# First attention of a fused graph kernel: layer-norm statistics of batches 2 to 7 made early, GpSimd's normalisations cut into pieces of three tiles

## What is computed

```python
x = x + _L0_gnn_ref(_layernorm(x, axis=-1), adj, L0_gnn_W, L0_gnn_a)      # the first attention
x = x + _L0_ffn_ref(_layernorm(x, axis=-1), ...)                          # 2 of 8 experts for each row
x = x + _L1_gnn_ref(_layernorm(x, axis=-1), adj, a0, a1, a2, a3)
x = x + _L1_ffn_ref(_layernorm(x, axis=-1), ...)

def _L0_gnn_ref(input, adj, W, a):
    h = jnp.matmul(input, W)
    f1, f2 = h @ a[:128, 0], h @ a[128:, 0]
    e = leaky_relu(f1[:, :, None] + f2[:, None, :], 0.2)
    attention = softmax(jnp.where(adj > 0, e, -9e15), axis=1)
    return elu(matmul(attention, h))
```

## Time and profile before

| | us |
|---|---|
| median of 3 runs | 1229.13 |
| lowest and highest run | 1223.91, 1231.8 |
| the profiled execution | 1227.33 |
| its span | 1225.6 |
| of it the loop of the first attention, from the first `shift` to the last | 34.3 to 315.0 |

### The profile page before, as it was taken

How to read it: one execution, slowest core, us unless ns; L and a number is a source line. 1 busy time by engine, 2 the same in 40 slices (tenths; PEclk the granted TensorE clock), 3 DMA queues, 4 the chain that set the end, 5 groups by cost and what they waited for, 6 DMA issues and landing times. The chain is left out here.

```text
span 1225.6 us, 17486 instructions
## 1 busy us (share of the span) xinstructions
PE 1119.4 (91%) x5314; PEld 672.3 (55%) x5346; DVE 671.1 (55%) x2158; ACT 743.4 (61%) x1063; POOL 414.1 (34%) x483
## 2 busy tenths in 40 slices
PE   2998898999619999969999999999799999999998
PEld 2554454444317777747777777777444444444443
DVE  4788987886634435436666667653253333333325
ACT  3887787786205554536666666666466666566661
POOL 6237777766755040434454555211000000000000
PEclk9898998998759999989999999999899999999999
DMA  8886765762134466422222222210000000000001
GB/s 260 319 322 217 276 215 211 254 233 108 39 126 130 140 191 190 141 78 78 80 79 79 78 79 81 66 52 11 1 0 9 9 17 9 18 9 9 18 9 35
DMA packets 69134, 130.98 MB, mean 107 GB/s; under 512 B 9918, under 2 KB 30764, under 8 KB 68012
## 3 DMA queue, kind: packets, MB, share of 16 engines
q1 hardware_dynamic: 60268, 111.96, 27.7%
q0 software_dynamic: 8192, 16.79, 4.6%
q10 hardware_dynamic: 576, 1.05, 0.2%
HBM read 77.60 MB, written 52.17 MB: 106 GB/s over the span
## 5 line engine op out<-in xcount | busy, mean ns | idle before, releaser
L1907 DVE CUSTOM_DVE_ANT_0 f_Y<-f_T,f_R 128x1024 f32<-128x1024 f32 x64 | 78.3, 1223 | 121.6 <-ACT f_R L1864 121.6
L2087 PE MATMUL eU<-XTN,V 128*128 128x512 f32 x256 | 133.5, 604 | 6.2 <-PEq L2021 6.2
L553 PE MATMUL O<-Y,HS 128*128 128x512 f32 x256 | 137.9, 660 | 0.0
L2095 PE MATMUL eU<-H,V 128*128 128x512 f32 x256 | 131.6, 596 | 0.0
L2103 PE MATMUL eY<-dGW,Vo 128*128 128x512 f32 x256 | 130.3, 596 | 1.3 <-DVE dGW L2294 1.2
L1746 POOL DMA_INDIRECT W<-sorted_y,ROW_I x96 | 91.5, 953 | 114.7 <-PE f_T L1807 96.6
L411 POOL DMA_INDIRECT sorted_x<-V,AT_I x112 | 110.6, 988 | 45.8 <-issue 29.7
L2194 ACT ACTIVATE H<-eU,bn 128x512 f32<-128x512 f32 x128 | 99.7, 779 | 39.5 <-PE eU L2087 32.5
L1827 PEld LDWEIGHTS f_O<-f_XN,f_PT 128*128 128x128 f32 x896 | 108.2, 192 | 17.8 <-issue 16.4
L1801 PE MATMUL f_T<-f_XT,f_XTA 128*128 128x512 f32 x224 | 114.6, 593 | 2.3 <-DVE f_XTA L1976 0.8
L1878 ACT COPY f_PT<-f_TP 128x512 f32<-128x512 f32 x128 | 68.8, 589 | 74.7 <-PE f_TP L1817 74.7
(11 more groups left out here) (281 smaller groups left out, 2011.8 us busy)
## 6 DMA issues: line engine op xcount, KB each, us to landing
ADJ<-in_adj SPq DMA_DIRECT2D x64, 512.0 KB, 5.1
masks<-NM SPq DMA_DIRECT2D x8, 2048.0 KB
f_MK<-masks SPq DMA_DIRECT2D x60, 256.0 KB, 2.7
sorted_y<-zero SPq DMA_DIRECT2D x39, 256.0 KB, 10.6
XB<-sorted_x SPq DMA_DIRECT2D x39, 256.0 KB, 2.7
sorted_y<-YB SPq DMA_DIRECT2D x39, 256.0 KB, 2.2
X<-in_x SPq DMA_DIRECT2D x8, 512.0 KB, 7.9
out_x<-X SPq DMA_DIRECT2D x16, 256.0 KB, 2.3
```

The source lines that it names most:

```text
L553: pe.matmul(O[:, h * HALF:(h + 1) * HALF], HS[:, g % 3, :], Y[:, g % 4, h * HALF:(h + 1) * HALF], start=False, stop=(c == NT - 1)).then_in ...
L1907: v.tensor_tensor_reduce(Y[:, g % 3, :], T[g % 2][:, :], R4[:, g % 2, :], -SLOPE, 3.0e38, ALU.add, ALU.min, LOW[:, g % RING:g % RING + 1]) ...
L2087: pe.matmul(U1[j % 2][:, :], V1[:, e * P:(e + 1) * P], XTN[:, b * N + q * HALF:b * N + (q + 1) * HALF], start=True, stop=True).then_inc(u1 ...
L2095: pe.matmul(U2[j % 2][:, :], V2[:, e * P:(e + 1) * P], H1[:, j % 2, :], start=True, stop=True).then_inc(u2_ready, 1)
```

## The change

LESS, SPREAD and ROOT get eight buffers in place of two, one per batch. The six `stats(2)` to `stats(7)` move: they stood in slot 1 of batches 0 to 5 (g = 1, 9, 17, 25, 33, 41) and now stand at g = 1, 3, 5, 7, 8 and 9. The wait of `stats` for `xn_ready` goes with the buffers.

On POOL, `norm(b + 2)` is cut: ROOT stays in slot 1, the eight tiles of XN go as three, three and two into slots 2, 3 and 4, behind the pair of scatters of each slot. `norm_r(b - 1)` is cut as well: `root_r` stays in slot 5, tiles 0 to 2 go to slot 6, 3 to 5 to slot 7, 6 and 7 to slot 0 of the next batch. The last `norm_r(7)` stays whole. No computation is added or left out.

```diff
-            LESS, SPREAD, ROOT, LESS_R, SPREAD_R, ROOT_R = (tile(n, [P, 2, NT]) for n in (
-                "LESS", "SPREAD", "ROOT", "LESS_R", "SPREAD_R", "ROOT_R"))
+            LESS, SPREAD, ROOT = (tile(n, [P, B, NT]) for n in ("LESS", "SPREAD", "ROOT"))
+            LESS_R, SPREAD_R, ROOT_R = (tile(n, [P, 2, NT]) for n in ("LESS_R", "SPREAD_R", "ROOT_R"))
...
-                def norm(b):
+                def root(b):
                     pool.wait_ge(mv_ready, b + 1)
-                    g_.tensor_tensor(ROOT[:, b % 2, :], SPREAD[:, b % 2, :], half8, ALU.pow).then_inc(pstep, 1)
+                    g_.tensor_tensor(ROOT[:, b, :], SPREAD[:, b, :], half8, ALU.pow).then_inc(pstep, 1)
                     pool.wait_ge(pstep, steps.next())
-                    if b >= 1:
-                        pool.wait_ge(xnt_ps[1], b)
-                    for t in range(NT):
...
+                def norm(b, tiles):
+                    for t in tiles:
+                        if t == 0 and b >= 1:
+                            pool.wait_ge(xnt_ps[1], b)
...
-                def norm_r(b):
-                    pool.wait_ge(root_ready, b + 1)
-                    if b >= 2:
-                        pool.wait_ge(sent[b % 2], b // 2 * EACH)
-                    for t in range(NT):
+                def norm_r(b, tiles):
+                    for t in tiles:
+                        if t == 0:
+                            pool.wait_ge(root_ready, b + 1)
+                            if b >= 2:
+                                pool.wait_ge(sent[b % 2], b // 2 * EACH)
...
                         send(sending, (2 * k, 2 * k + 1))
+                    if c == 0 and b >= 2:
+                        norm_r(b - 2, (6, 7))
                     if c == 1 and b + 2 < B:
-                        norm(b + 2)
+                        root(b + 2)
+                    if c in (2, 3, 4) and b + 2 < B:
+                        norm(b + 2, ((0, 1, 2), (3, 4, 5), (6, 7))[c - 2])
                     if c == 5 and b >= 1:
                         root_r(b - 1)
-                        norm_r(b - 1)
+                    if c in (6, 7) and b >= 1:
+                        norm_r(b - 1, ((0, 1, 2), (3, 4, 5))[c - 6])
...
                 send(LAST - 2, (2 * NT - 2, 2 * NT - 1))
+                norm_r(LAST - 1, (6, 7))
...
                 def stats(b):
                     moments(b)
-                    if b >= 2:
-                        dve.wait_ge(xn_ready, b - 1)
...
-                    if c == 1 and b + 2 < B:
-                        if b == 0:
-                            dve.wait_ge(x_rest, 16 * (B - 2))
-                        stats(b + 2)
+                    if g == 1:
+                        dve.wait_ge(x_rest, 16 * (B - 2))
+                    if g in (1, 3, 5, 7, 8, 9):
+                        stats((1, 3, 5, 7, 8, 9).index(g) + 2)
```

## The result

Before, in this comparison: 1228.32 us median (1223.73 to 1235.8, 20 runs). After: 1233.22 us (1226.89 to 1243.55, 20 runs). The ratio is 1.0042, 95% interval 1.0022 to 1.0062: slower by some 5 us, inside the 1% that I called "same" and inside the range, but on the other side of zero from the forecast of -1.7. The profiled execution has a span of 1229.5 us against 1225.6.

The account below looks back on a forecast made before the run. TensorE, busy 91% of the span, was taken to bound the kernel, with VectorE nearly as full in the loop. The terms -5.76 + 0 + 3.79 + 0.3 = -1.67 us took the 1229.13 median to 1227.5, range 1220.5 to 1236.

Parts of the forecast that it names:

- the 1% that I called "same": Whole kernel: a change within about 1%, 12.3 us, can't be told from none; chance of "same" 0.92.
- Part 3: POOL's norms in pieces: 0 in the loop, covered by POOL's idle time; +0.3 us in the tail.
- the Trainium skill's rule on the port: VectorE and GpSimd lock a shared port pair; read as longer cut tiles on POOL, up to +1.4 us in the tail.
- Part 1: `stats` leaving slot 1 of batches 2 to 5: -5.76 us in batches 4 and 5, 1.20 pacing and 4.56 clock.
- "0" for batches 2 and 3: Removing `stats` there is worth 0: the `shift` behind waited anyway, and the clock falls begin in untouched waits.
- Part 2: Four more `stats` between slots 3 and 9: 10.04 us of VectorE work less 6.25 idle, +3.79 us.
- no `shift` from 5 to 9 waits: Sign of being right: no `shift` from 5 to 9 waits for R.
- a sign against itself: A low clock between 50 and 80 us would show the forecast wrong.
- The tail: POOL's work up to `root_r(7)`, with `norm_r(6)` cut in three: +0.3 us, bounds -0.5 and +1.4.
- the estimated 0.1 for each start: In the tail, three starts of `norm_r(6)` in place of one cost an estimated 0.1 us each.
- A: Clock falls in batches 0 and 1, or batches 4 and 5 keep theirs: slower, 1232.0 to 1235.0 us; chance 0.30.
- B with Part 2 fully hidden: All clock falls go, batches 2 and 3 included (1222.3 us, chance 0.20); with the added `stats` hidden too, -10.3.

Follow-up runs that it names:

- e13: The changed kernel measured once more on a chip at 1229: ratio 1.0044 to the kernel before; its loop took 291.8 us.
- e1: The changed kernel with POOL's two norms whole again, only the statistics early: 4.8 us faster than the kernel before, ratio 0.9961.
- e17: Early statistics with both norms whole, measured again on another chip, at 1229: 1.5 us faster than the kernel before, ratio 0.9988.
- e2: The changed kernel with `stats` put back to slot 1, only POOL's norms in pieces: 3.4 us slower than the kernel before.
- e4: The kernel before without statistics 4 to 7, norms using those of batches 2 and 3: 0.66% faster, 8.1 us.
- e14: The changed kernel with the second norm whole in slot 5, the first in pieces, on a chip at 1229: level with the kernel before.
- e16: The changed kernel with the scatters of slots 2 and 3 held back, six in a row in slot 4: ratio 1.0018 to the kernel before.
- e3: The kernel before with four more sets of statistics added into a spare tile, nothing taken away: 0.44% slower, 5.4 us.
- e8: Early statistics, norms whole, later batches' statistics in halves in slots 1 and 3: 26.30 us from shift 3 to 10; no gain in time, chip at 1254.
- e12: The changed kernel with the first norm whole, the second in pieces, on a chip where the kernel before took 1259; the text gives no time.

## Why the prediction was wrong, step by step

The loop by groups of batches, each trace against the trace of before, in us (batch 7 up to its last `shift`):

```
batches             0, 1    2, 3    4, 5     6       7     loop
forecast            +3.8     0      -5.8     0       0     -2.0
changed kernel      +4.9    -0.6    -3.3    +1.0    -0.5   +1.5
  again (e13)       +8.2    -0.7    -3.3    +5.7    +1.3  +11.1
early alone (e1)    +5.4    -3.2    -4.3    +0.2    -3.2   -5.1
  again (e17)       +4.1    -3.2    -4.3    +0.2    -3.2   -6.4
```

**Part 3, "In the loop I count 0": this step failed.** It asked only whether anybody waits for POOL's results, and nobody does. But the pieces put a tile right behind a scatter 27 times between the start of batch 2 and the last `shift`, where the kernel before and e1 never do, and small operations of VectorE beside such a scatter take 0.52 in place of 0.17 to 0.23. These are on the path: they make H's parts and CH. Read against e1, slot 4 costs 0.64 more in two batches, slot 7 0.36 to 0.57 in five. In batch 4, where no trace of either kernel has a low clock, that leaves 35.36 and 35.37 (after, e13) against 34.52 and 34.51 (e1, e17). TensorE waits 9.2 us for CH from batch 2 to the last `shift` in place of 6.5 in e1, and more low clock comes with it: 27.3 and 50.8 us of the loop in the two traces with pieces, 17.1 and 23.5 in e1 and e17. How much of the clock is due to the pieces is not shown. Behind early statistics the pieces cost 7 to 10 us on the chips at 1230 (1.0042 and 1.0044 against 0.9961 and 0.9988, intervals that touch at most), each ratio against before on its own chip; the two kernels never ran side by side on such a chip. Alone the pieces cost 3.4 (e2), not clear of zero.

The prediction had the Trainium skill's rule on the port that VectorE and GpSimd share ("SBUF — State Buffer", SBUF: two separate sides) in hand and turned it one way only, to longer tiles on POOL. The trace shows the other: the 32 XN tiles of batches 2 to 5 took 18.6 us together where they took 20.2 before, and VectorE's operations were held. That the shared port is the cause no run shows.

**Part 1, batches 4 and 5 (-5.76): right for batch 4, too large for batch 5.** The falls of the clock in slot 3 of both batches (187.6 and 225.1 us in the trace of before) are gone with the `stats` of slot 1, as forecast, and e4 shows the full amount. With early statistics, however, another fall comes in slot 0 of batch 5: 212.3 to 215.8 us in e1, 211.0 to 214.4 in e17, 215.4 to 218.8 in the changed kernel. Batch 5 then takes 36.36 in e1 and 36.31 in e17, not 34.70. So some 1.6 us of this term failed without the pieces, and 0.8 in batch 4 through them. Why that fall comes is open: e14 and e16, with early statistics too, do not have it.

**"0" for batches 2 and 3: a right number by luck.** 75.59 before, 74.96 after. e1 shows what is under it: the earlier statistics alone bring 3.2 us there, and the pieces take 2.5 of them back.

**Part 2, four more `stats` (+3.79): right.** From shift 3 to shift 10 it is 3.7 after, 3.5 in e1, 3.3 in e3, and no `shift` from 5 to 9 waits. Batches 0 and 1 together grew by more, 4.9, with the two falls of the clock (54.9 and 72.0 us) that the prediction had named as a sign against itself.

**The tail (+0.3): nothing.** POOL took 25.49 for 25.54, inside the bounds; no run shows the estimated 0.1 for each start. VectorE waited 5.19 for `root_r(7)`, and 5.00 in e1, whose POOL works as before, so the longer wait does not come from the pieces.

**Parts 1 and 2 alone** are e1: -1.97 by their sum, -4.8 and -1.5 measured (e1, e17).

**The rivals.** A's time held, 1232.0 to 1235.0 with 1233.2 measured, but by luck. Its condition was a fall in batches 0 and 1, and one came in each; they cost e1 as much, and e1 was faster than before. Nothing on record priced VectorE's operations beside POOL's new places, and that is the rival that was missing. One sum is off by a little: B with Part 2 fully hidden is -10.6, not -10.3, which changes no chance.

## What to carry to other kernels

When work is moved on an engine that nobody waits for, list what it will now run beside on the other engines, above all short operations on the path, and price the overlap from a place in the trace where the two already meet. By the count here a tile is better placed elsewhere than right behind a scatter; that was not tried. And a change of half a per cent is to be judged on more than one chip: here the same two kernels came out at +0.4 and at -1.0%.

The best version depends on the comparison: early statistics with whole norms is 0.1 to 0.4% under before at 1230 and, by way of before, 0.5 to 0.8% under the changed kernel; early statistics with the second norm in 2, 3 and 3 tiles is 0.9 to 1.5% under before at 1254 to 1259. e8's halves on a chip at 1230, and pieces put ahead of the pair of scatters, which by the count above should leave VectorE's operations alone, were not tried.

## What the runs showed of the chip that I had not expected

- A small VectorE operation (128x8 to 128x64 elements) that begins 0.3 to 0.5 us after the start of a scatter on POOL takes about 0.52 us in place of 0.17 to 0.23 if a POOL tile follows that scatter directly (over 0.38 us in 26 of 31), and under 0.38 if not (85 of 85).
- On two of the chips, updates of semaphores by TensorE reach the waiting engine up to some 6 us after the instruction that gives them, in the slots behind six to eight scatters issued 1.27 us apart; on the chips at 1230 the same runs bring no delay. On those two the kernel before is 22 to 31 us slower; how much of that the late updates make is not shown.
- The granted clock fell at 287.0 after a wait of TensorE of 2.11 us, and in e1 at 212.3 after one of 1.27 (at 209.88); in e12 it did not fall in the slot of a wait of 2.30. The length of one wait does not tell. And the loop's low stretches differ between traces of the same kernel: 27.3 us in one of the changed kernel, 50.8 in another, e13.
